# AdaLN + MoE-LoRA feed-forward: the last batch stored by halves, its stores dealt to two queues, its last pair added singly

## What is computed

```python
cond  = x @ W.T + b + 2 * (x @ A_slot) @ B_slot      # LoRA slot by batch
logits = cond @ route_w.T                            # 8 experts
route  = one_hot(argmax(logits)) * max(logits)
h      = cond @ A.T                                  # 8 experts x rank 16 = 128 columns
out    = (route[..., None] * h) @ Bw                 # back to 2048 features
y      = x + out
```

## Time and profile before

| | |
|---|---|
| median of three runs | 295.32 us |
| the profiled execution, its own time | 294.95 us |
| its span (first to last recorded work) | 293.0 us |
| TensorE busy | 284.9 us, 97% |
| VectorE busy | 203.8 us, 70% |
| ScalarE busy | 114.1 us, 39% |
| HBM read / written | 54.60 MB / 33.55 MB |
| issues of the 256 KB stores at L270 | 16, median 2.8 us from issue to landing |

### The profile page before, as it was taken

The page is one execution under the profiler, slowest core; times in us unless marked ns, Lnnn a source line. Parts: engine busy times, 40 slices in busy tenths (PEclk is TensorE's granted clock), DMA queues, the critical chain, the costliest instruction groups (busy, mean ns, idle before and its releaser), DMA issues.

```text
span 293.0 us, 4467 instructions
## 1 busy us (share of the span) xinstructions
PE 284.9 (97%) x1740; PEld 228.0 (78%) x1740; DVE 203.8 (70%) x238; ACT 114.1 (39%) x167; POOL 11.9 (4%) x39
## 2 busy tenths in 40 slices
PE   7999999999999999999999999999999999999992
PEld 4999999996756885888588768857885887887992
DVE  0033200087697989789788969896897898898883
ACT  0200300296866432734373354427342732432500
POOL 7102100000000000000000000000000000000000
PEclk9999999999999999999999999999999999999999
DMA  7999999999970247859958993998499579455577
GB/s 239 408 391 406 415 411 411 375 414 422 420 303 0 91 198 255 319 169 405 388 188 304 395 368 147 359 377 346 154 389 385 221 272 419 171 233 235 193 250 240
DMA packets 21351, 88.52 MB, mean 302 GB/s; under 512 B 2378, under 2 KB 8914, under 8 KB 13522
## 3 DMA queue, kind: packets, MB, share of 16 engines
q1 hardware_dynamic: 18464, 85.79, 76.0%
q10 hardware_dynamic: 2866, 2.45, 2.5%
HBM read 54.60 MB, written 33.55 MB: 301 GB/s over the span
## 4 chain that ended last, share of the span: by engine, by line
PE 87%; DMA 5%; DVE 3%; SPq 2%; issue 1%; ACT 0%; DVEq 0%
PE bank_out L573 13%; PE bank_h L647 10%; PE bank_e L632 10%; PE bank_out L613 10%; PE bank_out L611 10%; PE bank_out L612 10%; PE bank_h L648 10%; PE bank_h L649 10%; DMA w_ring<-W 5%; DVE x_ring L520 2%; SPq L229 1%; PE bank_l L587 1%; DVE x_lo L425 1%; PE bank_r L666 1%; PE bank_r L573 1%
## 5 line engine op out<-in xcount | busy, mean ns | idle before, releaser
L337 ACT ACTIVATE x_hi<-x_ring 128x1024 fp32r<-128x1024 f32 (+1 forms) x72 | 68.9, 966 | 67.2 <-PE bank_h L649 66.8
L425 DVE TENSOR_TENSOR x_lo<-x_ring,x_hi 128x1024 fp32r<-128x1024 f32 (+1 forms) x72 | 79.1, 1104 | 15.5 <-ACT x_hi L337 15.5
L520 DVE TENSOR_TENSOR x_ring<-bank_out,x_ring 128x1024 f32<-128x1024 f32 (+1 forms) x72 | 79.1, 1101 | 0.6 <-PE bank_out L613 0.5
L647 PE MATMUL bank_h<-x_hi,m_hi 128*128 128x512 f32 (+1 forms) x144 | 54.1, 376 | 0.0
L613 PE MATMUL bank_out<-wh_hi,bw_lo 128*128 128x512 f32 (+1 forms) x144 | 53.3, 370 | 0.0
L611 PE MATMUL bank_out<-wh_hi,bw_hi 128*128 128x512 f32 (+1 forms) x144 | 53.3, 370 | 0.0
L648 PE MATMUL bank_h<-x_lo,m_hi 128*128 128x512 f32 (+1 forms) x144 | 53.3, 370 | 0.0
L612 PE MATMUL bank_out<-wh_lo,bw_hi 128*128 128x512 f32 (+1 forms) x144 | 53.1, 369 | 0.0
L649 PE MATMUL bank_h<-x_hi,m_lo 128*128 128x512 f32 (+1 forms) x144 | 53.1, 369 | 0.0
L573 PE MATMUL bank_out<-pt,w_ring 128*128 128x136 f32 x384 | 46.4, 281 | 1.1 <-DMA w_ring<-W 0.6
L573 PEld LDWEIGHTS bank_out<-pt,w_ring 128*128 128x128 f32 x384 | 45.4, 191 | 2.6 <-DMA w_ring<-W 2.4
(11 more groups left out here) (73 smaller groups left out, 170.7 us busy)
## 6 DMA issues: line engine op xcount, KB each, us to landing
x_ring<-xT SPq DMA_DIRECT2D x32, 1024.0 KB, 7.6
outT<-x_ring SPq DMA_DIRECT2D x28, 1024.0 KB, 4.8
w_ring<-W SPq DMA_DIRECT2D x31, 512.0 KB, 11.2
outT<-x_ring SPq DMA_DIRECT2D x16, 256.0 KB, 2.8
x_ring<-loraB ACTq DMA_DIRECT2D x8, 128.0 KB, 9.2
la<-loraA ACTq DMA_DIRECT2D x8, 128.0 KB, 13.4
x_ring<-BwT SPq DMA_DIRECT2D x1, 1024.0 KB, 10.5
pt<-PT SPq DMA_DIRECT2D x3, 272.0 KB, 7.3
```

The costliest lines, as they stand in the source:

```text
L337: act.activation(out, in_, ACT.Copy).then_inc(done, 1)
L425: dve.tensor_tensor(out, a, b, ALU.subtract).then_inc(done, 1)
L520: dve.tensor_tensor(x, out_banks(u, j), x, ALU.add).then_inc(v_out, 1)
L647: mm(h, m_hi[:, c, :], hi, start=(c == 0), stop=False)
```

## The change

The last batch is laid out by its halves: in HBM its four pieces become [half, piece of 8 chunks, partition, 8 chunks of 256 tokens]. Pieces 28 and 29 belong to unit 7, pieces 30 and 31 to unit 8, each still 8 KB on every partition and loaded with one transfer of 1024 KB. A pair of these units is then one run of 2 KB on each partition, in the ring as in HBM. The stores of unit 8 are dealt out: even pairs are issued by SP, odd ones by ACT, after its last copy. The last pair b7 is written to two banks (chunk 0 where it was, chunk 1 in `bank_h`), each chunk signals and is added by itself, and each is stored by itself with 128 KB: chunk 0 by ACT, chunk 1 by SP. The reshaping is also done in the host's packing and unpacking of `xT` and `outT`, which is not timed.

```diff
-        x_ring = sb("x_ring", [P, XRING, PC, T])
+        x_ring = sb("x_ring", [P, XRING, PIECE])
...
+        def x_piece(u, j):
+            b, t0, nt = UNITS[u]
+            return NQ * b + (C * t0 + 2 * nt * j) // PIECE
+
         def x_pair(u, j):
-            b, t0, nt = UNITS[u]
-            k = NQ * b + 2 * j // PC
-            return x_ring[:, k % XRING, 2 * j % PC:2 * j % PC + 2, t0:t0 + nt]
+            nt = UNITS[u][2]
+            at = 2 * nt * j % PIECE
+            return x_ring[:, x_piece(u, j) % XRING, at:at + 2 * nt].rearrange("p (c t) -> p c t", c=2)
...
+        def last_banks(i):
+            return bank_h[:, 0:UNITS[-1][2]] if i == 1 else out_banks(NU - 1, NP2 - 1)[:, 0, :]
...
+        def store_single(eng, i):
+            u, j = NU - 1, NP2 - 1
+            nt = UNITS[u][2]
+            at = 2 * nt * j % PIECE + i * nt
+            k = x_piece(u, j)
+            eng.wait_ge(v_out, NP2 * NU - 1 + i + 1)
+            eng.dma_start(outT[k, :, at:at + nt], x_ring[:, k % XRING, at:at + nt]).then_inc(d_last, 16)
+
+        def store_pair(eng, u, j):
+            nt = UNITS[u][2]
+            at = 2 * nt * j % PIECE
+            k = x_piece(u, j)
+            eng.wait_ge(v_out, NP2 * u + j + 1)
+            eng.dma_start(outT[k, :, at:at + 2 * nt], x_ring[:, k % XRING, at:at + 2 * nt]).then_inc(d_last, 16)
...
             for u in range(NB - 1, NU):
-                b, t0, nt = UNITS[u]
                 for j in range(NP2):
-                    sp.wait_ge(v_out, NP2 * u + j + 1)
-                    q, c = 2 * j // PC, 2 * j % PC
-                    sp.dma_start(outT[b, q, :, c:c + 2, t0:t0 + nt], x_pair(u, j)).then_inc(d_last, 16)
+                    if u < NU - 1 or j % 2 == 0:
+                        store_pair(sp, u, j)
+            store_single(sp, 1)
             for s in range(XRING):
                 sp.wait_ge(d_out[s], 16 * len(range(s, LAST, XRING)))
-            sp.wait_ge(d_last, 16 * NP2 * (NU - NB + 1))
+            sp.wait_ge(d_last, 16 * (NP2 * (NU - NB + 1) + 1))
...
                 copy(wh_hi[u % 2][:, 0:nt], wh[:, 0:nt], a_wh)
+            for j in range(1, NP2 - 1, 2):
+                store_pair(act, NU - 1, j)
+            store_single(act, 0)
...
-            for j in range(NP2):
+            for j in range(NP2 - 1):
                 add_x(NU - 1, j)
+            for i in range(2):
+                x = x_pair(NU - 1, NP2 - 1)[:, i, :]
+                dve.wait_ge(t_out, NP2 * NU - 1 + i + 1)
+                dve.tensor_tensor(x, last_banks(i), x, ALU.add).then_inc(v_out, 1)
...
-                    out = out_banks(u, j)[:, i, :]
+                    out = last_banks(i) if (u, j) == (NU - 1, NP2 - 1) else out_banks(u, j)[:, i, :]
...
-                last.then_inc(t_out, 1)
+                    if i == 1 or (u == NU - 1 and j == NP2 - 1):
+                        last.then_inc(t_out, 1)
...
-                        if c % PC == 0:
-                            x_landed(pe, NQ * b + c // PC)
+                        if c % 2 == 0 and (c == 0 or x_piece(u, c // 2) > x_piece(u, c // 2 - 1)):
+                            x_landed(pe, x_piece(u, c // 2))
```

More of the change, by code:

```diff
@@ L47, in adaln_ffn @@
 def adaln_ffn(nc, xT, slot_of, W, PT, bias, loraA, loraB, BwT, outT):
-    NB, NQ, _, PC, T = xT.shape
-    C = NQ * PC
+    NPIECES, _, PIECE = xT.shape
+    NWB, NWH, _, WO, WI = W.shape
+    NB = slot_of.shape[1]
+    C = NWH * WO
     NP2 = C // 2
-    NWB, NWH, _, WO, WI = W.shape
+    NQ = NPIECES // NB
+    PC = C // NQ
+    T = PIECE // PC
     E = 8
@@ L69, in adaln_ffn @@
     DONE = [max(n for n in range(NWP) if ORDER[n][0] == blk) + 1 for blk in range(NWB)]
-    NPIECES = NB * NQ
     assert ER == P and WI == 2 * P and NWB == NP2 and NB * R == P and BIAS_ROW < GROUP
@@ L90, in adaln_ffn @@
         assert WRING == 2 * SRING and WO * WI == 2 * T
-        x_ring = sb("x_ring", [P, XRING, PC, T])
-        lb = x_ring[:, 8, :, :].rearrange("p c t -> p (c t)").rearrange("p (b c r) -> p b c r", b=NB, c=C)
-        bw_raw = x_ring[:, 9, :, :].rearrange("p c t -> p (c t)")
-        lb_cols = x_ring[:, 11, :, :].rearrange("p c t -> p (c t)").rearrange("p (c b r) -> p c b r", b=NB, c=C)
+        x_ring = sb("x_ring", [P, XRING, PIECE])
+        lb = x_ring[:, 8, :].rearrange("p (b c r) -> p b c r", b=NB, c=C)
+        bw_raw = x_ring[:, 9, :]
+        lb_cols = x_ring[:, 11, :].rearrange("p (c b r) -> p c b r", b=NB, c=C)
         EARLY = (8, 9, 11)
@@ L237, in load_x @@
                     sp.wait_ge(v_bw, 1)
-                sp.dma_start(x_ring[:, slot, :, :], xT[k // NQ, k % NQ]).then_inc(d_x[slot], 16)
+                sp.dma_start(x_ring[:, slot, :], xT[k]).then_inc(d_x[slot], 16)
             def store(k):
                 sp.wait_ge(v_out, (k + 1) * (PC // 2))
-                sp.dma_start(outT[k // NQ, k % NQ], x_ring[:, k % XRING, :, :]).then_inc(d_out[k % XRING], 16)
+                sp.dma_start(outT[k], x_ring[:, k % XRING, :]).then_inc(d_out[k % XRING], 16)
             for n in range(NWP):
@@ L354, in split_hi @@
                     act.wait_ge(t_main, g - SRING + 1)
-                x_landed(act, NQ * b + 2 * j // PC)
+                x_landed(act, x_piece(u, j))
                 copy(x_hi[:, g % SRING, :, 0:nt], x_pair(u, j), a_xhi)
@@ L685, with pieces, unpieced @@
     c, pc, wblock, wo = d // P, 4, 2 * P, 4
+    def pieces(a):
+        whole = a[:-1].reshape(-1, P, pc * t)
+        halves = a[-1].reshape(c // pc // 2, 2, P, pc, 2, t // 2).transpose(4, 0, 2, 1, 3, 5)
+        return np.concatenate([whole, halves.reshape(-1, P, pc * t)])
+    def unpieced(a):
+        whole = a[:-(c // pc)].reshape(nb - 1, c // pc, P, pc, t)
+        halves = a[-(c // pc):].reshape(2, c // pc // 2, P, 2, pc, t // 2).transpose(1, 3, 2, 4, 0, 5)
+        return np.concatenate([whole, halves.reshape(1, c // pc, P, pc, t)])
     arrays = {
-        "xT": x.reshape(nb, t, c // pc, pc, P).transpose(0, 2, 4, 3, 1),
+        "xT": pieces(x.reshape(nb, t, c // pc, pc, P).transpose(0, 2, 4, 3, 1)),
         "slot_of": slot_of.reshape(1, nb),
@@ L702 @@
     got = run_bass_kernel_spmd(nc, [arrays], core_ids=[0]).results[0]["outT"]
-    return np.ascontiguousarray(got.transpose(0, 4, 1, 3, 2).reshape(nb, t, d))
+    return np.ascontiguousarray(unpieced(got).transpose(0, 4, 1, 3, 2).reshape(nb, t, d))
```

## The result

| | before | changed |
|---|---|---|
| median, 8 runs each | 295.23 us (294.15 to 295.52) | 293.86 us (293.61 to 295.08) |
| ratio, 95% interval | 1 | 0.9957 (0.9940 to 0.9974) |
| profiled execution, span | 294.95, 293.0 us | 295.08, 293.1 us |

The forecast was 294.05 us in a range of 293.1 to 295.0, and the median of 293.86 lies in it. The reason that the profiles show is that the start of phase 2 moves from execution to execution by more than the change is worth. It began at 69.9 us before and at 70.7 us after. The rows are of the line of the narrow matmuls, the first of which opens phase 2; first and last start stand after the durations (before, then after).

What follows compares the result with a forecast made beforehand. TensorE bounds until 287.6 us, then backlogged stores and one late DMA engine. Gap 0.4 and packet size 0.8, other parts 0, summed to 1.27 off the 295.32 us median: 294.05 us, range 293.1 to 295.0.

Steps and rivals of the forecast that it cites:

- What bounds the end: After TensorE ends at 287.59 us, backlogged stores remain; one DMA engine, 1.0 to 1.1 us behind, ends the kernel.
- the stall of SP's issue: SP's issue of b3 at 285.50 us took 1.25 us against 0.37, as if its queue had no room.
- The sum: Last packet at 290.98 instead of 292.25 us, a gain of 1.27, subtracted from the 295.32 us median.
- The gap: DMA share of 0.22 near 286.8 us, from a queue without room; expected to vanish, worth -0.4 us.
- the late engine: The DMA engine that fetched code near 285.4 us stays 1.05 us behind the fifteen; last packet at 290.98 us.
- The term of the 2 KB packets: Last stores at 383 GB/s instead of 341, 0.684 us a pair; worth 0.8 us.
- loads and layout of x: Last four x pieces: TensorE never waited there, so nothing gained and nothing later; 0.
- two queues: Unit 8's stores split between SP and ACT: no gain from this edit, no price in mixing.
- singles: Last pair added and stored by single chunks: hidden behind the backlog, 0; worth 0.3 to 0.4 us without one.
- B: Stores held at 341 GB/s by their destination, or runs still cut at 1 KB: gain 0.5, 294.8 us; chance 0.22.
- D: DMA engines taking turns between two store queues cost more: +0.5 at 300 GB/s, 295.8 us; chance 0.05.
- C: Code fetch falls before the kernel's end or is absorbed, no late engine: gain 2.3, 293.0 us; chance 0.11.

Runs made afterwards that it cites:

- e8_shift_before: Kernel before with 6 warm-up matmuls cut into 48 small ones, moving the code fetch earlier: last matmul to span end 4.11 us against 5.39; whole time 295.00 us, taken once.
- e2_queues: Kernel before with odd pairs of unit 8 issued by ACT, still 1 KB packets: last matmul to span end 5.37 us against 5.39.
- e6_blocks: Changed kernel with each pair of the last batch written as one 256 KB block in HBM: last matmul to span end 5.06 us.
- e9_blocks_shift: Changed kernel with 256 KB blocks and 48 small warm-up matmuls: 293.35 us against 295.35 before, ratio 0.9932; last matmul to span end 3.31 us.
- the repetition: Changed kernel again, unedited, on another chip beside its parts: no whole-time difference found from the kernel before; last matmul to span end 4.74 us against 5.39.
- e10_one_queue: e9_blocks_shift with all stores, the two last single chunks too, issued by SP: last matmul to span end 3.32 us.
- e1_layout: Kernel before with only the layout by halves, all stores from SP, last pair whole: last matmul to span end 4.79 us against 5.39.
- e7_shift_all: Changed kernel with 6 warm-up matmuls cut into 48 small ones, moving the code fetch earlier: last matmul to span end 4.33 us against 4.74.
- e5_swapped: Changed kernel with output pieces 30 and 31 exchanged in HBM: b0 fell from 73.6 to 53.8 ns per KB, b4 to b6 rose to 47 to 50.

## Why the prediction was right, and where it was off

**What bounds the end.** Right: a backlog of stores, with one engine a code fetch behind the others. It is shown by removal (`e8_shift_before`) and by the marks of b0. The fetch explains the stall of SP's issue and the hole of 0.4 us as well, since all three go when it is moved.

**The sum.** The forecast was -1.27 us; the tail gave -0.64, and both terms of the sum were off. The gap, "-0.4", was worth nothing: `e2_queues` closed it and the last packet ended 0.02 us earlier. By the forecast's own picture it could be worth no more, because the gap was idle time of the fifteen, and the kernel ends with the sixteenth. To "let the engines run without it" and keep the lag at 1.05 counts the gap as gained for the late engine too. In fact the lag grew by what the fifteen gained, from 0.92 to 1.29 us.

The term of the 2 KB packets, "nine pairs at 0.684 are 6.16", was mis-sized. With the gap it had the fifteen engines 1.2 us earlier; they were 0.2 to 0.4 earlier (3.66 to 3.46 and 3.30). The rate itself was right for most pairs (386 to 393 GB/s against 383), and b0 and b1 missed it: 73.6 and 63.9 ns per KB instead of 42 are 16 KB for each engine times 31.6 and 21.9, 0.86 us. I had interpolated between rates over packet size alone and had taken the write pattern for neutral; `e6_blocks` shows that it is not. Where blocks are written and no engine is late, the 0.8 forecast for packet size is what is measured (`e9_blocks_shift` against `e8_shift_before`, 0.80).

**The late engine.** The forecast was that the fetch "costs its engine the same 1.0 us" and that the lag is "kept at 1.05". Before, the fetch set the engine back by 1.9 us, of which 0.92 was left at the end. In the changed kernel the lag at the end was 0.48 and 0.64. I take it that the slow stretch, which held up the fifteen, let this engine catch up; no run shows that by itself. A correct size of the packet term would not have given 1.27 either: with the fifteen at full speed the lag was 1.69 (`e6_blocks`), and the tail got longer than the changed kernel's.

**The whole time.** That 293.86 came out so near to 294.05 is in good part luck: of the 1.37 us between the medians the tail accounts for 0.64, half of what was forecast, and the repetition had 0.0 with an interval of ±0.5. The mechanism of the gain is shown for the tail, not for the whole time. I had taken 0.2% as what a comparison can tell; with a start of phase 2 that scatters over 1.7 us, a comparison of 8 to 12 runs tells hardly less than that, and the change lies at it.

**The parts costed at nothing** were nothing: loads and layout of x (217.7 us from the start of phase 2 to the last matmul everywhere), two queues, singles. ACT's issues cost 0.34 to 0.86 us and hid as forecast. The singles ran as worked out, 0.77 us later in this execution: the first was to start at 287.53 and started at 288.30, the second was to end at 288.29 to 288.37 and ended at 289.04.

**The rivals.** B (packet size is not what costs) had a gain of 0.5, nearer to the tail's 0.64 than the forecast's 1.27, but not its reason: the rate did rise after the slow stretch. D (turns between two queues) is refuted by `e10_one_queue`, and for the slow stretch by `e1_layout`. C (no late engine) did not happen by itself; brought about in `e7_shift_all`, it gave 1.06 us over the kernel before and not 2.3.

**Two rules weighed before.** The Trainium skill (DMA: Bandwidth & Descriptors, "Why small descriptors are slow (HBM only)") would give 2 KB packets 4% over 1 KB ones, an estimate from its overhead of about 3 cycles for each packet. Stretches without any disturbance have 385 GB/s in `e9_blocks_shift` and 340 in `e8_shift_before`, 13%. The measurement decides, and it is three times what the rule gives. The same page of the Trainium skill, "Issuing engines are not separate DMA queues", has spreading the issues save only the sequencer's time. `e2_queues` and `e10_one_queue` agree: tails of 5.37 against 5.39 and 3.32 against 3.31 us.

Open: why it is b0 and b1, and what in HBM they meet. In `e5_swapped` b0 followed a7 at piece 31's place instead of piece 30's, and was less slow, so what is written just before may play a part. The pitch of 8 KB from row to row is not enough by itself: the kernel before has it too, with two runs of 1 KB in each row, and none of its stores is slow (47 to 50 ns per KB); nor is a4, the first pair of piece 29, in the changed kernel (42 to 43). No run here separates the pitch from what else was in flight.

## What to carry to other kernels

When a kernel ends in a backlog of stores, look at the last microseconds of the DMA row for a share near 1/16: it is one engine that lost time to something else, here a code fetch, and the end waits for it alone. Then count only what that engine gains: closing a hole in the work of the others won nothing, and moving the fetch by shifting the program was worth more in the tail (1.28 us) than making the packets larger (0.60). Estimate a transfer's rate from its run length and from the pattern in which it is laid down in HBM, and write blocks where the output's layout is free. Where phases before the edit scatter by more than the edit is worth, measure from a fixed event, here the last matmul, and not the whole time.

## What the runs showed of the hardware

- A fetch of 16 KB of program code is recorded as one packet of 0.95 to 1.47 us. In the kernel before it took 1.00 us and set its engine back by 1.9. It cost the tail 1.28 us with 1 KB stores (5.39 to 4.11) and 1.75 with 2 KB blocks (5.06 to 3.31).
- SP's issue stalled (1.25 us for 0.37) while one of sixteen engines was behind, and the others ran dry for 0.4 us (share 0.22); with the fetch moved the longest issue was 0.39 us.
- Stores reached 338 to 348 GB/s in 1 KB runs and 364 to 393 in 2 KB runs, but 242 to 258 for 1.5 us when the first two pairs of unit 8 were written as 2 KB rows 8 KB apart. With the same bytes in blocks of 256 KB that stretch had 376 to 385.
